# Weighted groups, projection and the maxima's split put in another order in an attention loop

## What is computed

```python
qkv = (x @ W_attn + b_attn).reshape(b, s, 3, H, HS)
q, k, v = (qkv[:, :, 0], qkv[:, :, 1], qkv[:, :, 2])
scores = jnp.einsum('bqhd,bkhd->bhqk', q, k) / scale
scores = jnp.where(causal, scores, -jnp.inf)
attn = jax.nn.softmax(scores, axis=-1)
out = jnp.einsum('bhqk,bkhd->bqhd', attn, v).reshape(b, s, H * HS)
return out @ W_proj + b_proj        # added to h
```

## Time and profile before

| | |
|---|---|
| median of 3 runs | 349.04 us (345.68 to 349.3) |
| span of the profiled execution | 347.3 us |
| PE busy | 279.1 us (80%) |
| PE weight loads busy | 209.5 us (60%) |
| DVE busy | 222.7 us (64%) |
| POOL busy | 196.4 us (57%) |
| ACT busy | 189.3 us (54%) |
| chain that ended last | PE 67%, DVE 6%, DMA 4%, ACT 3%, POOL 1% |

### The profile page before, as it was taken

How to read it: one execution, slowest core, us unless ns; L and a number is a source line. 1 busy time by engine, 2 the same in 40 slices (tenths; PEclk the granted TensorE clock), 3 DMA queues, 4 the chain that set the end, 5 groups by cost and what they waited for, 6 DMA issues and landing times.

```text
span 347.3 us, 8076 instructions
## 1 busy us (share of the span) xinstructions
PE 279.1 (80%) x2638; PEld 209.5 (60%) x2638; DVE 222.7 (64%) x1126; ACT 189.3 (54%) x393; POOL 196.4 (57%) x419
## 2 busy tenths in 40 slices
PE   0489130037899889999999999999999999999874
PEld 0356020036697757767767776776776677886663
DVE  1014010023568786988889889889888888866882
ACT  3425000016454585686586586586577467658762
POOL 3705777600001366866776676686686686556652
PEclk9958755559999999999999999999999999999986
DMA  5601311100056083464454355355244233000028
GB/s 141 192 14 31 85 20 20 20 2 0 25 126 124 17 125 95 71 114 101 76 106 110 73 96 120 78 84 133 69 92 115 94 82 116 3 4 2 1 84 280
DMA packets 26721, 27.28 MB, mean 79 GB/s; under 512 B 6834, under 2 KB 26416, under 8 KB 26680
## 3 DMA queue, kind: packets, MB, share of 16 engines
q1 hardware_dynamic: 23176, 23.69, 29.9%
q0 software_dynamic: 1568, 2.36, 3.0%
q10 hardware_dynamic: 1936, 0.72, 0.9%
HBM read 4.34 MB, written 3.15 MB: 22 GB/s over the span
## 4 chain that ended last, share of the span: by engine, by line
PE 67%; another core or an unknown queue 12%; DVE 6%; DMA 4%; ACT 3%; issue 3%; SPq 2%; POOL 1%; POOLq 0%; DVEq 0%; ACTq 0%
PE bank L1311 7%; PE bank L1345 7%; PE bank L1367 7%; PE bank L1249 4%; PE bank L1268 4%; PE bank L1307 3%; PE bank L1349 3%; PE bank L1285 3%; PE bank L1287 3%; PE bank L1257 3%; PE bank L1370 3%; PE bank L1228 2%; PE bank L1240 2%; SPq L296 2%
## 5 line engine op out<-in xcount | busy, mean ns | idle before, releaser
L857 DVE CUSTOM_DVE_ANT_0 C<-bank,MASKV 128x256 bf16<-128x256 f32 (+1 forms) x384 | 112.4, 350 | 17.9 <-PE bank L1311 14.0
L572 ACT ACTIVATE PT<-bank 128x512 f32<-128x512 f32 x144 | 80.0, 606 | 45.0 <-PE bank L1345 43.5
L372 POOL TENSOR_SCALAR_AFFINE_SELECT PT<-PT 128x256 f32<-128x256 f32 x144 | 66.3, 473 | 0.0
L350 POOL TENSOR_TENSOR PART<-RES,PART 128x256 bf16<-128x256 f32 (+1 forms) x31 | 27.9, 902 | 34.3 <-ACT PART L566 34.3
L368 POOL TENSOR_TENSOR CARRY<-CARRY 1x1 f32<-1x1 f32 x96 | 17.6, 183 | 46.4 <-ACT PT L572 46.4
L345 POOL DMA_INDIRECT G<-x,I x32 | 30.2, 944 | 21.0 <-PE bank L1157 11.6
L1228 PE MATMUL bank<-RH,LH 128*128 128x192 f32 x64 | 13.8, 359 | 26.0 <-ACT LH L509 24.2
L857 DVE DVE_READ_ACCUMULATOR2_ANT MX<- 128x1 f32 x384 | 31.9, 83 | 0.1
L805 DVE TENSOR_TENSOR RH<-bank,BFB 64x384 f32<-64x384 f32 x8 | 4.5, 560 | 41.5 <-remote 32.0
L1367 PE MATMUL bank<-PT,VA 128*32 128x256 f32 x384 | 30.7, 390 | 0.1
L1311 PE MATMUL bank<-KS,QS 96*128 96x256 bf16 x144 | 27.9, 275 | 1.0 <-DVE MX L857 0.8
(11 more groups left out here) (167 smaller groups left out, 648.7 us busy)
## 6 DMA issues: line engine op xcount, KB each, us to landing
QS<-PART SPq DMA_DIRECT2D x72, 96.0 KB, 3.6
KS<-PART SPq DMA_DIRECT2D x72, 96.0 KB, 3.4
out<-HT SPq DMA_DIRECT2D x7, 384.0 KB, 3.4
KSL<-PART SPq DMA_DIRECT2D x24, 96.0 KB, 3.3
QSL<-PART SPq DMA_DIRECT2D x24, 96.0 KB, 3.6
G<-x,I POOLq DMA_INDIRECT x42
out<-HT SPq DMA_DIRECT2D x2, 192.0 KB, 3.4
WFS<-wft ACTq DMA_DIRECT2D x2, 144.0 KB
```

What stands on the lines that cost most here:

```text
L350: pool.tensor_tensor(parts(b)[2][:, ROUNDS[w], :], RES[:, ROUNDS[w], :], parts(b)[1][:, ROUNDS[w], :], ALU.subtract).then_inc(p2_ok, 1)
L372: pool.affine_select(out=e, in_=e, compare_op=ALU.is_ge, fill=0.0, base=0, pattern=[[0, n], [1, P]], channel_multiplier=-1).then_inc(cut_o ...
L572: nc.scalar.activation(PT[:, v, :], BANK[T_BANK[(SU * par + v) % 2]][:, :], ACT.Exp, scale=SCALE).then_inc(exp_ok, 1)
L857: ins = nc.vector.tensor_tensor_reduce(JUNK[:, n:n + keys], bank[:, j * keys:(j + 1) * keys], MASKV[:, S - keys:S], 1.0, LOWEST, ALU.add, ...
```

## The change

For steps 1 to 12 (in the code `b.off < B - 3`, with B = 16; the loop's `step` runs to 13) two orders are changed; nothing is added or removed, and no wait's count is changed. On PE the end of the step becomes s7, st7, projection, s8, st8, w0, w1, w2, maxima. On POOL the mask of unit 8 goes ahead of the split of the maxima. Step 1 has no projection. Steps 13 to 15 keep the old order.

```diff
-                max_parts(b)
+                if b.off >= B - 3:
+                    max_parts(b)
                 if not b.first:
                     causal(b - 1, 2, 1)
+                if b.off < B - 3:
+                    max_parts(b)
...
-                weighted(d, 1 - par, 0)
-                scores(b, par, 8)
-                scores_t(d, 1 - par, 8)
-                if b.off >= 2:
+                if b.off < B - 3:
+                    if b.off >= 2:
+                        project(b - 2)
+                    scores(b, par, 8)
+                    scores_t(d, 1 - par, 8)
+                    weighted(d, 1 - par, 0)
+                    weighted(d, 1 - par, 1)
+                    weighted(d, 1 - par, 2)
+                    max_t(b)
+                else:
+                    weighted(d, 1 - par, 0)
+                    scores(b, par, 8)
+                    scores_t(d, 1 - par, 8)
                     project(b - 2)
-                weighted(d, 1 - par, 1)
-                max_t(b)
-                weighted(d, 1 - par, 2)
+                    weighted(d, 1 - par, 1)
+                    max_t(b)
+                    weighted(d, 1 - par, 2)
```

## The result

| | before | after |
|---|---|---|
| median of 4 runs on one chip | 348.62 us (345.68 to 349.3) | 357.15 us (354.66 to 358.23) |
| ratio after to before, 95% interval | | 1.0366 (1.0308 to 1.0423) |
| span of the profiled execution | 347.3 us | 356.5 us |

The changed kernel is slower: by 2.4% in the medians, by 2.6% in the spans of the two profiled executions, and by 3.7% in the ratio, which compares faster executions alone and comes out higher than the runs listed here account for. The forecast was 358.2 us within 353 to 362, and 356.4 us for the span.

A forecast was written before the change was run, and what follows sets the result against it. PE was taken as the bound: per step 0.78 + 0.33 us of waits less 0.23 us saved by grouping, 0.88 us. Eleven steps, 9.7 us, less 0.55 in step 1, give 9.1 us: 358.2 us, range 353 to 362.

The forecast's parts named there:

- The wait for bank 6: PE at the moved projection, steps 2 to 12: stands still 0.78 us until DVE's `rest` has read bank 6; bounds 0 and 0.78.
- The end of `rest`: DVE's read of bank 6: stays where it is against the step's start, 8.99 us.
- Group 2 waits: PE ahead of w2: a second pause of 0.33 us for POOL's mask of unit 8; bounds 0.1 and 0.33.
- up to 0.5 us: Group 2's pause on PE would be longer by up to this without POOL's new order of mask and split.
- The pause on DVE: DVE, steps 2 to 12: was to move from before the residual to before the maximum of unit 8.
- DVE's three pauses: DVE in step 7: 0.62, 0.17 and 0.79 us; gaining all three would give the projection's wait its lower bound, 0.
- the split's end: POOL at the step's end: split of the maxima runs behind the select from 207.41 for under 0.5 us, ready at 207.95.
- the reaction of PE: PE's start after another engine's end: 0.06 us, taken from a group behind a mask, added to the wait's end at the projection.
- step 1: No projection there; group 2 gets its mask earlier, so step 2 starts 0.55 us earlier.
- The first: Rival: the projection doesn't wait; 0.10 us more per step, 349.6 us, no change; 5 in 100.
- The second: Rival: maxima come late too, each next step's st0 waits; another 0.8 us per step, 367 us; 3 in 100.
- The third: Rival: the array's mode changes cost more than starts show, 0.40 us each; a step gains 0.5 us, 343 us; 4 in 100.

The follow-up runs named there:

- e1: Changed kernel with the read of bank 6 (ACT's and DVE's parts) one unit earlier in steps 1 to 12: 350.32 us, ratio 1.0124, step 12.88 us.
- e2: Kernel before with the same earlier read of bank 6 on ACT and DVE: 349.3 us, ratio 1.0101, step 12.87 us.
- e8: Changed kernel with six of the twelve transfers for step 2 issued by SP in step 0, ahead of the first maxima: 357.94 us in one run.
- e9: Kernel before with the projection alone moved right behind st7, ahead of w0, in steps 2 to 12: 372.5 us in one run, step 14.76 us.
- e3: Changed kernel with the projection back behind st8, groups together and POOL's new order kept: 351.03 us, ratio 1.0116, step 12.79 us.
- e7: Kernel before with only w1 and w2 put together behind the projection, and POOL's new order: 350.35 us, ratio 1.0016, step 12.75 us.

## Why the prediction came out

**What it had right.** The wait for bank 6 is there with its releaser, in eleven steps, and e1 with its control e2 shows that the read's place alone makes it. The end of `rest` stays 8.99 us behind the step's start. Projection to s8 takes 1.37 us, st8 to w0 0.32 against 0.30, the groups stand 0.67 us apart against 0.68, the transposition takes 0.21 us to the next step, and no wait stands ahead of it. Group 2 waits 0.33 us, as predicted, and without POOL's new order it is 0.35 us longer, within the "up to 0.5 us". The pause on DVE moved where it was to move. Two slips in the working did no harm: of DVE's three pauses, which were to bound the wait from below, the one of 0.79 us stands behind `rest`, and the other two happen to add up to 0.79 us as well; and the terms of the split's end add up to 207.91, not 207.95.

**The term that was mis-sized in steps 2 to 12** is the projection's wait: 0.88 us for 0.78. The end of `rest` was right; the reaction of PE was taken as 0.06 us, from a group of matmuls that a POOL mask let go, and here it is 0.15 us. PE's weight loads in the changed kernel, of the projection and of group 2:

```profile
207.92 0.62 PEld L1288 LDWEIGHTS bank<-WP,ONT 128*128 128x128 f32 x4 [0.97 <-issue]
...
211.54 0.16 PEld L1370 LDWEIGHTS bank<-PT,VA 128*32 128x32 f32 x8 [0.43 <-POOL PT L372]
```

`rest` ends at 207.81, the load starts 0.11 us later and the matmul at 207.96. Behind the mask that ends at 211.49 both start 0.05 us later. A step became 0.96 us longer by this, instead of 0.88; over eleven steps that is 0.9 us. The sum over steps 2 to 12 shows only 0.2 us of it, since steps 4 and 12 of the kernel before were 0.3 us longer than the others, which the prediction, made from step 7, left out.

**The step that failed** is step 1: -0.55 us predicted, +0.44 measured. PE's part of it was right to 0.01 us, and in e8, without the wait for the transfers, step 1 takes 12.25 us against the 12.24 us predicted. What failed is that the next step's start was said to depend on PE's work alone; the bracket `[0.21 <-issue]` in the earlier trace rows was there to be seen, and 0.09 us ahead of that start the last keys had landed: it was the wait for them. That the span came out to 0.1 us is luck: step 1 took 0.99 us more than predicted, and the stretch ahead of it, which the change doesn't touch, was 0.94 us shorter.

**The rivals.** The first (the projection doesn't wait, no change) is refuted by the bracket. What it said of such a kernel can be read from e1 against e2: 0.01 us per step where it gave 0.10. The second (each next step's st0 waits for the maxima) did not come: in step 7 of the changed kernel st0 starts at 202.65 without a bracket. In e9 the maxima do come late, but there the transposition itself waits, for ACT's copy to XNT. The third (the changes of mode cost much more than starts show) is refuted: from st7 to the next step's start the changed kernel takes 5.57 us, without its two waits (0.88 and 0.33 us) 4.36 us, against 4.61 us before, so the grouping gives PE 0.25 us per step (0.23 was predicted), where 1.11 us were needed. The Trainium skill says in "TensorEngine Tiling (Array Packing)", Tiling Modes, that a change of tiling mode drains the engine, while a change of tile does not. The trace agrees in the direction: 0.67 us from group to group against 0.79 us from a group to a score unit, and 0.32 us from a unit to a group against 0.22 us to a unit, so 0.10 to 0.12 us for each change. No run here shows that it is the drain that takes this time.

**Steps 13 and 14.** That step 13 lost 0.33 us and step 14 gained 0.35 us can be read from the traces. In the changed kernel step 14 starts at 293.38, behind a bracket of 0.27 us without a name and 0.09 us behind the last landing of its keys (293.29): the wait of step 1 again. The transposition of step 12 now stands at that step's end, so SP issues the first transfer of step 13 at 1.26 us after its start instead of 0.20. In the kernel before, step 14 had a wait of 0.32 us for the transfer of the maxima; now only the weight load of st0 waits for it, 0.3 us, and st0 comes 2.82 us behind the transposition (292.12 to 294.94), against 2.84 us before. What step 13 waits longer, step 14 waits less.

**What stays open** is what stretches an issue of SP, and with it shifts the last landing by up to half a microsecond and more. The traces point to the loading of instructions, whose packets they list under two queues of their own (q8 and q14). In the eleven traces from 110 us on, no issue of these transfers that started clear of such a packet took more than 0.60 us (1583 issues); of the 269 that met one, 64 took more than 0.8 us, and up to 2.06 us. No run tests it.

## What to carry to other kernels

Before an instruction is moved forward on the engine that bounds, look at what it waits for and at what stood ahead of it: the work that it overtakes was the cover of its wait, and the whole wait comes onto the path, once per step. A second wait then appears where the delayed work is needed next, so follow the chain through every engine to the step's end; an order on another engine can be worth 0.36 us in that state and cost 0.09 us without it. And a step whose start shows a small idle time with no engine named may already be held by something else, here a transfer, and then a gain on the engine ahead of it does not arrive.

## What the runs showed of the hardware

- The time from the end of the releasing instruction to PE's matmul differs with the pair: 0.05 us from POOL's select to a weighted group, 0.07 us from DVE's read of the maximum to s8 (e3), 0.14 us from ACT's copy to the transposition (e9), and 0.15 us from DVE's `rest` to the projection. The weight load starts 0.05 to 0.06 us after the first two and 0.11 us after the other two. What decides it was not tested.
- The loop has a second bound just below PE's: the transfers of the queries and keys, twelve per step at some 0.62 us of SP each, and 3.1 to 4.0 us (medians by tile) from issue to landing. The kernel before meets it in steps 4 and 12 (12.97 and 12.98 us instead of 12.64: the next step starts 0.09 us after the last landing in both, and in each one issue of SP took much longer, 1.37 and 2.04 us), and e3 and e7 more often. In steps 2 to 12 of the changed kernel the last landing comes 0.59 us or more ahead of the next start, and nothing waits for it.
